# Extraction of the largest values in one block of eight units, with the ratios behind its first round and the clipping behind the block

## The chip, the cores and the metric

The kernel runs on one core of one Trainium2 chip. The metric is the device time of one execution in microseconds (us). PE is TensorE, DVE VectorE, ACT ScalarE, POOL GpSimd, SP SyncE. Each engine works through its own queue in order and waits at semaphores.

## The reference, cut to what matters

Four layers of a graph network run over 64 graphs of 256 nodes with 128 features, with one dense 256x256 adjacency for each graph; each layer adds to `x`:

```
h = relu(layernorm(x)); x = x + L0(h, adj)   # normalised adjacency, elu
h = relu(layernorm(x)); x = x + L1(h, adj)   # hyperbolic attention: logmap, expmap
h = relu(layernorm(x)); x = x + L2(h, adj)   # per edge: gelu(layernorm(m_j + m_i + b1)), summed with adj
h = relu(layernorm(x)); x = x + L3(h, adj)   # four stacked layers, row and column norms of adj
```

Two parts concern the change. L1 needs `_atanh(sn)` for every pair of nodes, with `sn` clipped below 1. The kernel takes it as a ratio by logarithms and exponentials: Ln of numerator and denominator, their difference, Exp of half of it, a clip, then Ln(1-u) and Ln(1+u). L2 sums over the edges of a node, and only about 3% of the entries of `adj` are not zero. So the kernel extracts for each node the list of its non-zero entries, eight at a time, and L2 runs over these slots and not over 256 neighbours.

## The kernel before, in words

Four graphs make a group, sixteen groups in all. A group has eight units: a unit is one half (128 rows) of one graph's adjacency. The main loop alternates two stages. `slots(g)` is the edge loop of L2 for group g, two slots in each turn. `mix(g)` does everything between two edge loops, each part for another group: the update after L2 of group g (flag `u`), L1 and the extraction for group g+1 (flag `l1`), L0 for group g+2 (`l0`), and L3 for group g-1 (`l3`). The order of the work on each engine is written out by hand in `mix`, once for each engine; nothing plans it.

The extraction is done sixteen times. This text calls these times block 0 to block 15. Blocks 0 and 1 stand in mixes without L3, block 15 in one without L0, the thirteen between in full mixes.

The extraction is `take_slots` (L1044) on DVE. One round, `eight` (L1054), takes the eight largest values of each unit (MAX8, L1056), finds their columns (L1059, a load of the values and FIND_INDEX8), copies the values away (L1060), overwrites them in `adj_x` (L1064, a load and MATCH_REPLACE8; not in the last round) and copies the columns away, cast to bf16 (L1065). A drain of DVE stands between these steps. The number of rounds is read from `n_slots`: three for fifteen blocks, four for block 3. It is the count of the first round, of a loop with a register bound, and of the last round.

Before, the extraction is made of two calls with four units each. In DVE's order (L1393 to L1402): the clamps of the last graph's pair terms (`clamp_pair`, `clamp_den`), then `take_slots(a, 0)` with all its rounds, then `ratios` (L1251), then `take_slots(a, 1, between=clip)`: its first round, `clip` (L1257), its further rounds. Then comes `index_ready`, then `layer0_z` (L997, from L1002 on), and `coefficients` (L1262).

- `ratios` is four subtractions 128x512 of two SBUF tiles (L1255), one for each graph. The one of graph b waits for ACT's Ln of that graph (L858) and for POOL's addition `total` (L584), which reads the same logarithms.
- ACT answers with Exp (L870, L871), and stands behind `keep_f` (L683) of L3 with it.
- `clip` is four operations 128x512 (L1260); each waits for one L870. After its own `keep_sd` copies (L679) ACT loads a table and waits for each `clip` before the Ln pair of that graph (L884, L885; "the artanh pair" below). Behind the four pairs ACT has a table load (L886), two `keep_f`, and `keep_index` (L699).
- PE's queue has at this place L3's products `l3_f(2, 0)` and `(2, 1)`, `turn_index` (L1702, matmuls L1710, waits for `index_ready`), `l3_f(2, 2)` (from L1612 on, waits for the first of those `keep_f`), `(2, 3)`, then `support` (L1692, waits for the result of `coefficients`, L1273).
- SP waits for `index_ready` to load `adj_x` for the next group.
- Later, `move` (L1310) on DVE waits for ACT's Tanh (L903), which stands in ACT's queue behind the last four `keep_sd`.

Of the kernel before, what the change touches and what calls it, by code (L numbers as in the profile page):

```python
# [32 lines left out]
GB = 4  # L33
# [177 lines left out]
UNITS = GB * NB  # L211
HALF = UNITS // 2
# [31 lines left out]
def network(nc, w, keep, out):  # L244
    with ExitStack() as stack:
# [11 lines left out]
        value = plan.sb("value", [P, UNITS, SLOTS])  # L257
# [3 lines left out]
        index = plan.view("index", [P, UNITS, CHUNKS * P], at, BF16)  # L261
# [66 lines left out]
        top = plan.sb("top", [P, UNITS, 8])  # L328
        top_at = plan.sb("top_at", [P, UNITS, 8], U32)
# [603 lines left out]
        def _(dve):  # L933
            v = nc.vector
# [62 lines left out]
            def layer0_z(z_):  # L997
                for b in range(GB):
                    dve.wait_ge(sem["out_made"], z_ * GB + (b // 2 * 2 + 2))
                    for k in range(NB):  # L1000
                        u = b * NB + k
                        v.scalar_tensor_tensor(z0[:, u], quarter(b)[:, k * P:(k + 1) * P],  # L1002
                                               norm[:, u:u + 1], bc["L0_gnn_b"][:], ALU.mult, ALU.add)
                dve.drain()
                for b in range(GB):
                    v.tensor_scalar(z0_low[:, of(b)], z0[:, of(b)], 0.0, None, ALU.min).then_inc(sem["z0_low_ready"], 1)
                v.scalar_tensor_tensor(normed[:], z0[:], 0.0, nodes(z_), ALU.max, ALU.add)
                dve.drain()
# [32 lines left out]
                v.tensor_scalar(n_slots[0:1, bass.ds(a, 1)], needed_g[:], 7.0, float(N), ALU.max, ALU.min)  # L1041
                dve.drain().then_inc(sem["slots_ready"], 1)

            def take_slots(a, part_, between=None):  # L1044
                units = range(part_ * HALF, (part_ + 1) * HALF)
                these = slice(part_ * HALF, (part_ + 1) * HALF)
                for b in range(part_ * 2, part_ * 2 + 2):
                    dve.wait_ge(adjx_in[b], a * 16 + 16)
                dve.wait_ge(sem["index_cleared"], a + 1)
                dve.sem_inc(keep["held"], 1)  # L1050
                n = dve.value_load(n_slots[0:1, bass.ds(a, 1)], min_val=7, max_val=N)
                full = dve.snap(((n + 1) // 2 * 2 + 10) // 8 - 1)

                def eight(r, more):  # L1054
                    for u in units:
                        v.max(top[:, u], adj_x[:, u])  # L1056
                    dve.drain()
                    for u in units:
                        v.max_index(top_at[:, u], top[:, u], adj_x[:, u])  # L1059
                    v.tensor_copy(value[:, these, bass.ds(r * 8, 8)], top[:, these])  # L1060
                    dve.drain()
                    if more:
                        for u in units:
                            v.match_replace(adj_x[:, u], top[:, u], adj_x[:, u], LOWEST)  # L1064
                    v.tensor_copy(index[:, these, bass.ds(r * 8, 8)], top_at[:, these])  # L1065
                    dve.drain()

                eight(0, True)
                if between:
                    between()  # L1070
                with dve.Fori(1, full) as r:
                    eight(r, True)
                eight(full, False)
# [68 lines left out]
            def mix(g, l1=True, l0=True, l3=True, u=True):  # L1142
                a, z_, t = g + 1, g + 2, g - 1
# [97 lines left out]
                def clamp_pair(b):  # L1241
                    dve.wait_ge(sem["pair_made"], a * GB + (b + 1))
                    v.tensor_scalar(pair[:, b, 0], bank_b[:, 0], -2.0, MIN_NORM, ALU.mult, ALU.max).then_inc(sem["square_ready"], 1)
                    dve.wait_ge(sem["square_ready"], a * GB + (b + 1))
                    v.tensor_tensor(pair[:, b, 1], pair[:, b, 0], bank_b[:, 1], ALU.add).then_inc(sem["pair_read"], 1)

                def clamp_den(b):
                    dve.wait_ge(sem["pair_read"], a * GB + (b + 1))
                    v.tensor_scalar(pair[:, b, 1], pair[:, b, 1], MIN_NORM, None, ALU.max).then_inc(sem["pair_clamped"], 1)

                def ratios():  # L1251
                    for b in range(GB):
                        dve.wait_ge(sem["ln_ready"], a * GB + (b + 1))
                        dve.wait_ge(sem["total_ready"], a * GB + (b + 1))
                        v.tensor_tensor(pair[:, b, 0], pair[:, b, 0], pair[:, b, 1], ALU.subtract).then_inc(sem["diff_ready"], 1)  # L1255

                def clip():  # L1257
                    for b in range(GB):
                        dve.wait_ge(sem["s_ready"], a * GB + (b + 1))
                        v.tensor_scalar(pair[:, b, 0], pair[:, b, 0], MAX_TANH, None, ALU.min).then_inc(sem["u_clipped"], 1)  # L1260
# [131 lines left out]
                if l1:  # L1392
                    clamp_pair(3)  # L1393
                    clamp_den(3)
                    take_slots(a, 0)
                    ratios()
                    take_slots(a, 1, between=clip)
                    dve.drain().then_inc(sem["index_ready"], 1)
                if l0:
                    layer0_z(z_)  # L1400
                if l1:
# [31 lines left out]
            for piece in (layer0_stats, layer0_eps, layer0_normed, layer0_scaled, layer0_z, layer0_moved, layer0_variance):  # L1433
                piece(0)
            mix(-1, l3=False, u=False)
            slots(0)
            mix(0, l3=False)
            with dve.Fori(1, GROUPS - 2) as g:
                slots(g)
                mix(g)  # L1440
# [493 lines left out]
```

## Time and profile before

| | |
|---|---|
| median of 3 runs | 4111.16 us (4110.72 to 4120.36) |
| the profiled execution's own time | 4122.07 us |
| its span, first to last instruction | 4120.2 us |
| busy PE / DVE / ACT / POOL | 87% / 83% / 68% / 52% |
| granted TensorE clock, mean | 0.923 |

The profiled execution lies 11 us above the median and 2 us above the highest of the three runs. A row of the time line gives the start in us from the span's start, the duration from the first start to the last end, engine, line, operation, output and inputs with their shapes, and the count; in brackets the idle time just before and what ended it.

### The profile page before, as it was taken

To read this page: it belongs to the slowest core of one execution; us is meant where nothing else is said; L and a number is where in the kernel's file an instruction comes from. 1 tells how busy PE (TensorE), PEld (TensorE's weight loads), DVE (VectorE), ACT (ScalarE), POOL (GpSimd) and SP (SyncE) were. 2 spreads that over 40 slices of the span, in tenths; PEclk is the share of its full clock that TensorE was granted. 3 is DMA by queue.
4 is the path that set the end of the run, shared out by engine and by line. 5 is a ranking of instruction groups with operands and counts; after the bars stand their busy time and mean duration, and the time that the engine had idled before them with its cause. 6 is when DMAs were issued, how large, how long until landed. Compare 5 with 4: busy or idle time off the path is not lost.

```text
span 4120.2 us, 103754 instructions
## 1 busy us (share of the span) xinstructions
PE 3577.9 (87%) x30351; PEld 3064.0 (74%) x30772; DVE 3411.6 (83%) x12271; ACT 2808.7 (68%) x6445; POOL 2154.7 (52%) x1987
## 2 busy tenths in 40 slices
PE   3494789889899999989899898998999898998998
PEld 2283778778787787868778786877878687786887
DVE  4788888898888888888888888888888888887840
ACT  2484776858667685866858686685858668595753
POOL 1182763719456382844728274572828447292730
PEclk7596889999998999989999898989989899999999
DMA  2000001000010100001010000101000010000000
GB/s 80 26 1 26 1 1 42 1 25 17 1 42 1 42 0 21 21 1 42 1 42 0 21 22 1 42 1 42 0 21 21 1 42 1 26 0 1 16 1 21
DMA packets 95517, 73.95 MB, mean 18 GB/s; under 512 B 7504, under 2 KB 95184, under 8 KB 95184
## 3 DMA queue, kind: packets, MB, share of 16 engines
q1 hardware_dynamic: 95184, 70.09, 5.6%
q8 instruction: 138, 2.26, 0.2%
q14 instruction: 195, 1.60, 0.1%
HBM read 61.68 MB, written 8.39 MB: 17 GB/s over the span
## 4 chain that ended last, share of the span: by engine, by line
PE 61%; DVE 16%; ACT 8%; issue 8%; POOL 3%; DVEq 2%; ACTq 0%; POOLq 0%; DMA 0%; SPq 0%
PE n_bank_d L1512 11%; PE n_bank_c L1501 9%; PE n_bank_b L1501 9%; PE n_bank_c L1598 9%; PE n_bank_d L1615 4%; PE n_bank_d L1616 4%; PE n_bank_d L1612 3%; PE n_bank_a L1484 3%; PE n_bank_b L1676 2%; DVE v_normed L987 1%; DVE v_normed L1149 1%; POOL v_z L517 1%; PE n_bank_a L1472 1%; DVE v_z L1109 1%; ACT v_pair L858 1%
## 5 line engine op out<-in xcount | busy, mean ns | idle before, releaser
L517 POOL TENSOR_TENSOR v_z<-v_z,all_bc_L_gnn_be 128x512 f32<-128x512 f32 x620 | 788.3, 1273 | 32.4 <-DVE v_z L1109 32.4
L1512 PE MATMUL n_bank_d<-v_diag,v_msg 128*128 128x128 f32 x4960 | 618.3, 278 | 25.1 <-ACT v_diag L756 25.1
L531 POOL TENSOR_TENSOR v_prstd<-v_pvar,all_neg_half 128x8 f32<-128x8 f32 x310 | 561.8, 1812 | 105.7 <-DVE v_pvar L1125 76.9
L1512 PEld LDWEIGHTS n_bank_d<-v_diag,v_msg 128*128 128x128 f32 x4960 | 577.0, 192 | 28.1 <-ACT v_diag L756 28.1
L756 ACT ACTIVATE v_diag<-all_ident,v_value 128x128 f32<-128x128 f32 x1860 | 573.6, 389 | 0.0
L1501 PEld LDWEIGHTS n_bank_b<-v_parts,v_onehot 128*128 128x128 bf16 x8208 | 473.4, 98 | 90.6 <-ACT n_bank_b L688 56.9
L1501 PE MATMUL n_bank_b<-v_parts,v_onehot 128*128 128x128 bf16 x8208 | 512.8, 219 | 26.2 <-ACT n_bank_b L688 26.1
L1501 PEld LDWEIGHTS n_bank_c<-v_parts,v_onehot 128*128 128x128 bf16 x7440 | 442.0, 100 | 108.9 <-ACT n_bank_c L688 64.6
L1501 PE MATMUL n_bank_c<-v_parts,v_onehot 128*128 128x128 bf16 x7440 | 479.8, 222 | 42.1 <-ACT n_bank_c L688 42.1
L1598 PE MATMUL n_bank_c<-all_l_wsd,v_fT 128*128 128x256 f32 x1792 | 457.8, 398 | 28.4 <-ACT v_adjT L673 25.9
L683 ACT ACTIVATE v_fT<-n_bank_d,all_l_c 128x256 f32<-128x256 f32 x256 | 120.0, 475 | 461.0 <-PE n_bank_d L1616 460.8
L1598 PEld LDWEIGHTS n_bank_c<-all_l_wsd,v_fT 128*128 128x128 f32 x1792 | 360.0, 201 | 69.9 <-issue 1.4
L751 ACT ACTIVATE v_msg<-v_z 128x512 f32<-128x512 f32 x620 | 384.0, 619 | 36.2 <-PE n_bank_d L1512 24.4
L1109 DVE SCALAR_TENSOR_TENSOR v_z<-n_bank_c,v_prstd,all_bc_L_gnn_g 128x128 f32<-128x128 f32 x1240 | 345.9, 345 | 66.5 <-PE n_bank_b L1501 36.1
L593 POOL TENSOR_TENSOR v_s_norm<-v_s_norm2c,v_half 128x8 f32<-128x8 f32 x16 | 28.1, 1758 | 710.7 <-DVE v_s_norm2c L1308 710.7
L692 ACT ACTIVATE v_spread<-n_bank_a 128x1024 bf16<-128x1024 f32 x342 | 345.0, 1009 | 60.0 <-PE n_bank_a L1484 42.9
L1109 DVE SCALAR_TENSOR_TENSOR v_z<-n_bank_b,v_prstd,all_bc_L_gnn_g 128x128 f32<-128x128 f32 x1240 | 346.9, 345 | 26.0 <-POOL v_prstd L531 25.8
L679 ACT ACTIVATE v_sd<-n_bank_c 128x512 f32<-128x512 f32 x256 | 151.0, 595 | 265.4 <-PE n_bank_c L1598 264.1
L1615 PE MATMUL n_bank_d<-v_adjT,v_sd 128*128 128x256 f32 x1024 | 327.9, 404 | 0.0
L1616 PE MATMUL n_bank_d<-v_adj_l,v_sd 128*128 128x256 f32 x1024 | 324.3, 400 | 0.0
L1099 DVE TENSOR_SCALAR v_onehot<-v_spread,v_node_of 128x1024 bf16<-128x1024 bf16 x684 | 307.8, 491 | 2.8 <-ACT v_spread L692 2.1
L1117 DVE BATCH_NORM_STATS2 v_pstats<-n_bank_b 128x6 f32<-128x256 f32 x620 | 234.2, 422 | 65.4 <-PE n_bank_b L1501 47.3
(283 smaller groups left out, 7435.5 us busy)
## 6 DMA issues: line engine op xcount, KB each, us to landing
v_adj_l<-in_adj SPq DMA_DIRECT2D x128, 256.0 KB, 3.6
v_adj_x<-in_adj SPq DMA_DIRECT2D x64, 256.0 KB, 3.5
v_ring<-in_x SPq DMA_DIRECT2D x16, 512.0 KB, 6.0
out_x<-v_xout SPq DMA_DIRECT2D x64, 128.0 KB, 1.9
w_wu<-in_L_gnn_wu SPq DMA_DIRECT2D x4, 192.0 KB, 2.5
all_W<-in_L_gnn_W SPq DMA_DIRECT2D x2, 128.0 KB, 4.0
w_raw<-in_L_gnn_ws SPq DMA_DIRECT2D x1, 192.0 KB, 3.0
w_raw<-in_L_gnn_wd SPq DMA_DIRECT2D x1, 192.0 KB, 3.2
```

The source lines that it names most:

```text
L517: nc.gpsimd.tensor_tensor(z[par][:, units], z[par][:, units], wide(bc["L2_gnn_be1"])[:, units], ALU.add).then_inc(sem["z_ready"], 1)
L531: nc.gpsimd.tensor_tensor(prstd[:], pvar[:], minus_half, ALU.pow).then_inc(sem["prstd_ready"], 1)
L692: nc.scalar.activation(spread[:], ps_spread, ACT.Copy).then_inc(sem["spread_kept"], 1)
L751: nc.scalar.activation(msg[par][:, units], z[par][:, units], ACT.Gelu).then_inc(sem["msg_ready"], 1)
L756: ins = nc.scalar.activation(diag[par][:, u], ident[:], ACT.Copy, scale=value[:, u, bass.ds(slot, 1)])
L1099: ins = v.tensor_scalar(onehot[:, par, k], spread[:], node_of[:, k:k + 1], None, ALU.is_equal)
L1109: ins = v.scalar_tensor_tensor(z[par][:, u], ps_m[par][:, u], prstd[:, u:u + 1], bc["L2_gnn_g1"][:], ALU.mult, ALU.mult)
L1501: ins = nc.tensor.matmul(ps_m[par][:, u], onehot[:, par, k, u * P:(u + 1) * P], parts[:, b * NB + k, t], start=False, stop=False, skip_gro ...
L1512: ins = nc.tensor.matmul(ps_agg[:, u // NB, (u % NB) * P:(u % NB + 1) * P], msg[par][:, u], diag[par][:, u], start=False, stop=False, skip ...
L1598: ins = nc.tensor.matmul(ps_l3[b % 2][:, k], fT[:, b, L3_SLOT[f], k * P:(k + 1) * P], keep["l3_wsd"][:, sum(L3_IN[:l]) + i, :], start=Fals ...
L1615: nc.tensor.matmul(acc, sd[:, b, k, 0:D], rowT[:, b, k], start=False, stop=False)
L1616: ins = nc.tensor.matmul(acc, sd[:, b, k, D:2 * D], colA[:, b, k], start=False, stop=k == NB - 1)
```

## The change

The two calls become one over all eight units. Each round now runs each of its steps over eight units, with the same number of MAX8, FIND_INDEX8 and MATCH_REPLACE8; its two copies move 64 elements a partition where they moved 32. There is one entry, one read of `n_slots` and one loop where there were two. `ratios` now runs behind the first round of the eight units, `clip` behind the whole block and behind `index_ready`. Nothing changes in the queues of ACT, PE, POOL and SP.

```diff
-            def take_slots(a, part_, between=None):
-                units = range(part_ * HALF, (part_ + 1) * HALF)
-                these = slice(part_ * HALF, (part_ + 1) * HALF)
-                for b in range(part_ * 2, part_ * 2 + 2):
+            def take_slots(a, between):
+                for b in range(GB):
                     dve.wait_ge(adjx_in[b], a * 16 + 16)
                 dve.wait_ge(sem["index_cleared"], a + 1)
                 dve.sem_inc(keep["held"], 1)
...
                 def eight(r, more):
-                    for u in units:
+                    for u in range(UNITS):
                         v.max(top[:, u], adj_x[:, u])
                     dve.drain()
-                    for u in units:
+                    for u in range(UNITS):
                         v.max_index(top_at[:, u], top[:, u], adj_x[:, u])
-                    v.tensor_copy(value[:, these, bass.ds(r * 8, 8)], top[:, these])
+                    v.tensor_copy(value[:, :, bass.ds(r * 8, 8)], top[:])
                     dve.drain()
                     if more:
-                        for u in units:
+                        for u in range(UNITS):
                             v.match_replace(adj_x[:, u], top[:, u], adj_x[:, u], LOWEST)
-                    v.tensor_copy(index[:, these, bass.ds(r * 8, 8)], top_at[:, these])
+                    v.tensor_copy(index[:, :, bass.ds(r * 8, 8)], top_at[:])
                     dve.drain()

                 eight(0, True)
-                if between:
-                    between()
+                between()
                 with dve.Fori(1, full) as r:
                     eight(r, True)
                 eight(full, False)
...
                     clamp_den(3)
-                    take_slots(a, 0)
-                    ratios()
-                    take_slots(a, 1, between=clip)
+                    take_slots(a, between=ratios)
                     dve.drain().then_inc(sem["index_ready"], 1)
+                    clip()
```

## Rows read from the trace of the kernel before

**Rows 1.** The page, part 4: the chain that ended last, by engine
```profile
PE 61%; DVE 16%; ACT 8%; issue 8%; POOL 3%; DVEq 2%; ACTq 0%; POOLq 0%; DMA 0%; SPq 0%
```
**Rows 2.** The waits, whole span: total us, times, longest
```profile
ACT v_s_th L903 <- DVE v_s_targ L1312: 34.7, 3, 17.3
```
**Rows 3.** Time line of DVE, block 2, first round of the first four units
```profile
599.50 1.41 DVE L1056 MAX8 v_top<-v_adj_x 128x8 f32<-128x256 f32 x4 [0.49 <-issue]
600.98 0.09 DVE L1059 MATCH_VALUE_LOAD v_top_at<-v_top,v_adj_x 128x8 f32 x1
...
602.81 0.09 DVE L1064 MATCH_VALUE_LOAD v_adj_x<-v_top,v_adj_x 128x8 f32 x1
...
604.39 0.18 DVE L1065 CAST v_index<-v_top_at 128x32 bf16<-128x32 uint32 x1
```
**Rows 4.** Time line of DVE, block 2, last round and what follows
```profile
633.12 1.41 DVE L1056 MAX8 v_top<-v_adj_x 128x8 f32<-128x256 f32 x4 [0.48 <-issue]
...
636.99 2.16 DVE L1002 SCALAR_TENSOR_TENSOR v_hn<-n_bank_a,v_norm,all_bc_L_gnn_b 128x128 f32<-128x128 f32 x8 [0.28 <-issue]
```
**Rows 5.** Time line of DVE, block 2, end of the first call, and ratios
```profile
613.76 1.19 DVE L1060 COPY v_value<-v_top 128x32 f32 x1
615.11 1.05 DVE L1065 CAST v_index<-v_top_at 128x32 uint32 x1 [0.17 <-issue]
616.31 2.50 DVE L1255 TENSOR_TENSOR v_pair<-v_pair 128x512 f32<-128x512 f32 x4
```
**Rows 6.** Time line of POOL, block 2
```profile
611.17 4.95 POOL L584 TENSOR_TENSOR v_total<-v_pair 128x512 f32<-128x512 f32 x4 [16.84 <-ACT v_pair L858]
```
**Rows 7.** Time line of ACT, block 2
```profile
636.23 0.63 ACT L884 ACTIVATE v_pair<-v_pair 128x512 f32<-128x512 f32 x1
...
641.82 0.84 ACT L683 ACTIVATE v_fT<-n_bank_d,all_l_c 128x256 f32<-128x256 f32 x2
```
**Rows 8.** Time line of PE, block 2
```profile
642.43 1.10 PE L1612 MATMUL n_bank_d<-v_fT,all_l_wn 128*128 128x256 f32 x4 [0.74 <-ACT v_fT L683]
...
647.69 1.95 PE L1692 MATMUL n_bank_b<-v_h,v_pair 128*128 128x129 f32 x16
```
**Rows 9.** Time line of DVE, block 2, the end of the coefficients
```profile
646.50 2.50 DVE L1273 TENSOR_TENSOR v_pair<-v_total,v_gate 128x512 f32<-128x512 f32 x4
```
**Rows 10.** Time line of DVE, block 0
```profile
130.65 1.41 DVE L1056 MAX8 v_top<-v_adj_x 128x8 f32<-128x256 f32 x4 [0.71 <-issue]
...
152.80 1.44 DVE L1260 TENSOR_SCALAR v_pair<-v_pair 128x512 f32<-128x512 f32 x4
...
163.82 2.16 DVE L1002 SCALAR_TENSOR_TENSOR v_hn<-n_bank_a,v_norm,all_bc_L_gnn_b 128x128 f32<-128x128 f32 x8 [0.19 <-issue]
```
**Rows 11.** Time lines of POOL, ACT, DVE and PE, block 3
```profile
844.73 4.97 POOL L584 TENSOR_TENSOR v_total<-v_pair 128x512 f32<-128x512 f32 x4 [15.46 <-ACT v_pair L858]
...
868.08 0.63 ACT L884 ACTIVATE v_pair<-v_pair 128x512 f32<-128x512 f32 x1
...
878.31 2.16 DVE L1002 SCALAR_TENSOR_TENSOR v_hn<-n_bank_a,v_norm,all_bc_L_gnn_b 128x128 f32<-128x128 f32 x8 [0.28 <-issue]
...
881.08 2.04 PE L1612 MATMUL n_bank_d<-v_fT,all_l_wn 128*128 128x256 f32 x4 [0.38 <-issue]
```
**Rows 12.** Time lines of POOL, ACT and DVE, block 4
```profile
1107.59 4.95 POOL L584 TENSOR_TENSOR v_total<-v_pair 128x512 f32<-128x512 f32 x4 [15.43 <-ACT v_pair L858]
...
1130.94 0.63 ACT L884 ACTIVATE v_pair<-v_pair 128x512 f32<-128x512 f32 x1
...
1131.72 2.16 DVE L1002 SCALAR_TENSOR_TENSOR v_hn<-n_bank_a,v_norm,all_bc_L_gnn_b 128x128 f32<-128x128 f32 x8 [0.27 <-issue]
```
**Rows 13.** Time lines of POOL, DVE and ACT, block 15
```profile
3761.88 4.95 POOL L584 TENSOR_TENSOR v_total<-v_pair 128x512 f32<-128x512 f32 x4 [19.11 <-ACT v_pair L858]
...
3765.79 3.40 DVE L1255 TENSOR_TENSOR v_pair<-v_pair 128x512 f32<-128x512 f32 x4
...
3784.10 0.63 ACT L884 ACTIVATE v_pair<-v_pair 128x512 f32<-128x512 f32 x1
```

## The prediction

> **What bounds the kernel now.** I read the page first, for the chain of work that ended last: PE carries 61% of it, DVE 16%, ACT 8% [rows 1]. No engine bounds the whole, so the change has to be read at its place. Second, the waits: of the sixteen Tanh that close a block's L1, only three waited for DVE, 34.7 us in all [rows 2]; in thirteen blocks DVE was ready when ACT had worked off its queue. The time lines say which three: blocks 0, 1 and 15. Third, the time lines of DVE, ACT, POOL and PE around one block, and the sixteen blocks laid side by side. Blocks 2 and 5 to 14 (eleven) repeat one pattern to about 0.1 us; block 2 stands for them. Blocks 0 and 1 are alike; 3, 4 and 15 are each their own.
>
> In block 2 the reader is to see a race between three queues. DVE ends the extraction at 636.71 (636.99 less the gap of 0.28) [rows 4]. ACT starts the artanh pairs at 636.23 and reaches the next `keep_f` at 641.82, 5.59 later [rows 7]. PE waits for it: it stood 0.74 until 642.43, and then ran through to `support` at 647.69 [rows 8]. DVE's first result for `support` was there at about 647.19 (646.50 plus 0.69, a quarter of the four in 2.50 with its tail) [rows 9], 0.5 ahead. So PE and ACT set the pace behind the block, and DVE keeps up with 0.5 to spare.
>
> **Part 1, the merged rounds.** A full round of four units takes 5.07: from 599.50 to the end of the cast at 604.57; MAX8 1.48, FIND_INDEX8 and the copy 1.83, MATCH_REPLACE8 1.58, cast 0.18 [rows 3]. One more unit costs 0.33 for MAX8 (four in 1.41, so 1.0 over three steps) and about 0.39 for each of the two pairs (1.58 over four). Eight units: 5.07 + 4 x 1.11 + 0.06 for the longer copies = 9.57, against 10.14 for two rounds of four. No row has a copy of 64 elements; it is bounded by 0.18, that of 32, and twice that, and I take the lower end and 0.03, as fixed cost rules rows this short; the upper end would add 1 us to a block. The last round takes 3.59 (633.12 to 636.71) [rows 4]: for eight units 3.59 + 4 x 0.72 + 0.05 = 6.52, against 7.18. The loop's exit costs 0.48 [rows 4]. What follows the ratios is then 9.57 + 0.48 + 6.52 = 16.57 with three rounds, 26.62 with four.
>
> Blocks 0 and 1 have no L3, the logarithms lie long ready, and DVE is what everyone waits for. From the first MAX8 to `layer0_z` is 33.17 now (130.65 to 163.82) [rows 10]. After: 9.57 + 2.40 (ratios, 0.60 each [rows 5]) + 16.57 + 1.44 (clips [rows 10]) + 0.19 = 30.17. That is 3.0 less in each. The clips come later there, but ACT's pairs (four in 4.2 by block 2's pace) are done before `coefficients` starts, 4.3 behind the last clip. Blocks 0 and 1: -6.0. If the drains and the loop's entry lay hidden already, it would be 0; that end goes into the range.
>
> **Part 2, the ratios move ahead of their inputs.** In block 2 the first round of eight ends at 599.50 + 9.57 = 609.07. POOL's additions, which the ratios wait for, start at 611.17 and run one after the other to 616.12, 1.24 apart [rows 6]; they hang on ACT's table load and Ln, which nothing here moves. So a stall of over 3 us opens on DVE where there was none, and then DVE is paced by POOL. Do the two engines run beside each other? In block 2 a copy and a cast beside the additions took 1.19 and 1.05 where the same forms take 0.17 and 0.18 [rows 3, 5], and in block 15 the four subtractions themselves, started 1.04 before the last addition ended (3766.83), took 3.40 where they take 2.50 [rows 5, 13]. DVE waited for the running addition to end. I take it so: the first subtraction waits until the second addition is done (2.48), runs 0.60, then they alternate: 2.48 + 0.60 + 1.24 + 0.60 + 1.24 + 0.60 + 0.60 = 7.36 from the first addition's start. Without such waits it would be 4.95 + 0.60 = 5.55.
>
> The Trainium skill says the same, in "SBUF — State Buffer", section "Who interferes with whom": a VectorE operation with two inputs in SBUF and a GpSimd operation that reads SBUF exclude each other for a whole instruction. By this rule the sum below holds; without it, it would be 5 us lower. The rows agree with it, for the cast and for the subtraction.
>
> Block 2: the ratios end at 611.17 + 7.36 = 618.53, now 618.81. What the stall costs, the merging and the absent clip waits give back. The extraction ends at 618.53 + 16.57 = 635.10, 1.6 earlier.
>
> **Part 3, the clip behind the block.** Its 1.44 come on top: `layer0_z` starts at 635.10 + 1.44 + 0.28 = 636.82, now 636.99: nothing won that counts. ACT's wait for the first clip takes the place of its wait for PE's copies: first clip done at 635.10 + 0.43 = 635.53, needed at 636.23 [rows 7], so 0.7 remains. That cover hides the move in these eleven blocks; if it is gone, each us costs one us of ACT, behind it of PE (`keep_f`, then `l3_f(2, 2)`, `support`, four `l3_sd`, the Tanh). `index_ready` comes 1.6 earlier, but `turn_index` stands behind L3 products in PE's queue, so no one is waiting; SP loads `adj_x` 1.6 earlier, needed a group later. Eleven blocks: 0 each.
>
> Where the cover is thinner:
> - Block 4. Ratios end 1107.59 + 7.36 = 1114.95, extraction 1131.52, first clip 1131.95; ACT would start at 1130.94 [rows 12]: 1.0 late. `layer0_z` at 1133.24, now 1131.72: 1.5 late, beyond DVE's 0.5. I take +1.5.
> - Block 15. Ratios end 3769.24, extraction 3785.81, first clip 3786.24, ACT now starts at 3784.10 [rows 13]: +2.1, for PE waits for `keep_f` there too.
> - Block 3, four rounds. Ratios end 852.09, extraction 878.71, first clip 879.14, where ACT starts at 868.08 now [rows 11], eleven us earlier. `keep_f` comes 5.59 after, ends at 885.15, and PE's product starts there and not at 881.08: +4.1. Part of it comes back, since these four matmuls took 2.04 after PE had stood still and 1.10 in block 2 [rows 8, 11]. DVE alone: `layer0_z` 880.43 for 878.31, +2.1. Between 2.1 and 4.1 I take +3.
>
> **Sum.** -6.0 + 0 + 1.5 + 2.1 + 3.0 = +0.6 us, on the profiled execution's 4122.07: 4122.7. That execution lies 10.9 over the median of the runs shown; carried over, 4111.16 + 0.6 = 4112. The edits cancel.
>
> **The rivals.**
> - No exclusion of the additions and subtractions. Ratios end 1.8 earlier. Blocks 4 and 15 then cost 0 and 0.3, block 3 1.3: sum -4.4, 4107. For it: only block 15 shows a late subtraction. Against it: 0.9 there is clear. Still "within".
> - DVE is the bound everywhere, and each block gives the 3.0 of block 0: -48, 4063. For it: DVE is 16% of the chain. Against it: rows 2 and 8, and the new stall of 3 us.
> - Slower: the clip comes late on ACT in all full blocks. Its place is the 0.7 before the first artanh pair. It decides as soon as the extraction ends over 0.7 later than worked out, through longer copies (the upper end, 1 us) and issue gaps of 0.5 at each of the steps as DVE shows them here and there. At 2 us later: 1.3 x 11 = 14, 2 x 3 = 6 in blocks 3, 4, 15, and 4 less won in blocks 0 and 1: +25, 4136. For it: the cover is thin, and thirteen blocks share it. Against it: each stage is scaled from its own row.
> - The change does not do what it says: drains and entries were hidden, blocks 0 and 1 give nothing: +6.6, 4118.
> - TensorE's granted clock falls at other places (2.04 against 1.10 for the same four matmuls is what it does): some 1 us a block, either sign.
>
> **How the numbers follow.** The forecast 0.60, with its own range 4105 to 4120; no exclusion 0.12; slower by a late clip 0.14; DVE the bound 0.05; nothing won 0.05; clock 0.04. About 0.3% (12 us) is what a measurement of this kernel can tell from no change. Slower by more: the 0.14 and 0.02 of clock and of the costs' upper ends, 0.16. Faster: 0.05 and 0.02, 0.07. Within: 0.77. The range reaches from the case without exclusion less the spread of the runs to the beginning of the late clip, 4102 to 4126.
>
> **What would show it.** DVE idle before L1255 of 3 us and more until POOL's L584 in the full blocks, and the four subtractions spread over some 6 us; none in blocks 0 and 1, which are 3 us shorter. MAX8 in rows of eight, 9.6 us a round. The first L884 unmoved against the `keep_sd` before it in block 2, late by 1 in block 4, by 2 in block 15, by 11 in block 3. Wrong would be: ACT idle before L884 in block 2 (then slower), the Tanh there earlier against the `keep_sd` (then faster), or subtractions of 0.69 each right behind their additions.

## The result, and the profile after

The changed kernel takes 4107.41 us (median of 12 executions, 4096.21 to 4114.05), the kernel before in the same rounds 4117.01. The ratio is 0.9974, its 95% interval 0.9966 to 0.9982: faster by 0.26%, some 10 us. I had forecast no change, 4112. The time lies in the range, and within the 0.3% that I called no change; but the interval of the ratio excludes 1, and where those 10 us come from is the question of what follows. That the number is only 5 off is in part luck: it rests on three runs with a median of 4111.16, and on the 4117.01 of the twelve my +0.6 would have given 4117.6. The profiled execution has a span of 4112.1 (before 4120.2), with the same mean clock of 0.923. Of all executions behind this text one, of the version with late ratios and 256 drains, was slow (4747.66 at a mean granted clock of 0.725), and no median or ratio below counts it.

The chain of the page, by engine, and the waits that answer to [rows 1, 2] (waited for: us in total, times, longest):

```profile
PE 58%; DVE 19%; ACT 7%; issue 7%; POOL 3%; DVEq 2%; POOLq 0%; ACTq 0%; DMA 0%; SPq 0%
```
```profile
DVE v_pair L1252 <- POOL v_total L584: 47.5, 14, 3.4
ACT v_pair L884 <- DVE v_pair L1257: 39.4, 6, 12.3
ACT v_s_th L903 <- DVE v_s_targ L1309: 30.6, 2, 15.4
...
PE n_bank_b L1706 <- DVEq L1393: 27.3, 3, 10.7
```

The first line is new: in each of fourteen blocks DVE stands 3.4 before the ratios until POOL's addition. The second was 1.5 in two waits; now ACT waits for the clip in six blocks. The lines of the changed kernel stand 2 to 5 lower in number than those of before, from the extraction on. Block 2 on DVE, against [rows 3 to 5]:

```profile
592.19 2.72 DVE L1054 MAX8 v_top<-v_adj_x 128x8 f32<-128x256 f32 x8 [0.58 <-issue]
...
598.15 0.18 DVE L1058 COPY v_value<-v_top 128x64 f32<-128x64 f32 x1
...
601.56 0.18 DVE L1063 CAST v_index<-v_top_at 128x64 bf16<-128x64 uint32 x1
605.15 5.63 DVE L1252 TENSOR_TENSOR v_pair<-v_pair 128x512 f32<-128x512 f32 x4 [3.40 <-POOL v_total L584]
610.70 2.70 DVE L1054 MAX8 v_top<-v_adj_x 128x8 f32<-128x256 f32 x8
...
627.04 0.20 DVE L1063 CAST v_index<-v_top_at 128x64 uint32 x1 [0.17 <-issue]
627.41 1.43 DVE L1257 TENSOR_SCALAR v_pair<-v_pair 128x512 f32<-128x512 f32 x4 [0.17 <-issue]
628.76 2.15 DVE L1002 SCALAR_TENSOR_TENSOR v_hn<-n_bank_a,v_norm,all_bc_L_gnn_b 128x128 f32<-128x128 f32 x8
```

One round of eight takes 9.55 (592.19 to 601.74; worked out as 9.57), and the copy of 64 elements costs what one of 32 did. POOL and ACT at the same place, ACT and PE in block 3, and ACT in block 5:

```profile
603.77 5.86 POOL L584 TENSOR_TENSOR v_total<-v_pair 128x512 f32<-128x512 f32 x4 [17.10 <-ACT v_pair L858]
```
```profile
627.88 0.63 ACT L884 ACTIVATE v_pair<-v_pair 128x512 f32<-128x512 f32 x1 [0.75 <-DVE v_pair L1257]
```
```profile
870.18 0.63 ACT L884 ACTIVATE v_pair<-v_pair 128x512 f32<-128x512 f32 x1 [11.00 <-DVE v_pair L1257]
```
```profile
870.38 1.84 PE L1706 MATMUL n_bank_b<-v_ident,v_index 128*128 128x128 bf16 x8 [6.16 <-DVEq L1393]
876.38 1.19 PE L1608 MATMUL n_bank_d<-v_fT,all_l_wn 128*128 128x256 f32 x2 [4.16 <-ACT v_fT L683]
```
```profile
1360.06 0.76 DVE L1257 TENSOR_SCALAR v_pair<-v_pair 128x512 f32<-128x512 f32 x2 [0.17 <-issue]
```
```profile
1361.46 0.63 ACT L884 ACTIVATE v_pair<-v_pair 128x512 f32<-128x512 f32 x1
```

The ratios end 7.01 after the first addition starts (610.78 less 603.77; worked out as 7.36), and the additions themselves are stretched from 4.95 [rows 6] to 5.86. In block 5 the first clip is done at about 1360.5, 0.95 ahead of ACT.

From the first MAX8 of a block to its Tanh, in the two profiled executions:

| block | before | after | measured | forecast |
|---|---|---|---|---|
| 0 | 59.59 | 57.07 | -2.5 | -3.0 |
| 1 | 59.40 | 56.42 | -3.0 | -3.0 |
| 3 | 71.52 | 75.04 | +3.5 | +3.0 |
| 4 | 62.08 | 63.40 | +1.3 | +1.5 |
| 15 | 62.55 | 65.92 | +3.4 | +2.1 |

These five sum to +2.7 where I had +0.6. In the steady blocks the time from the first addition to the Tanh is 51.98 for 52.09. So by its own edits the change gives nothing, as forecast, and the profiled execution is still 8 us shorter. Laid side by side over the sixteen blocks, these 8 are: -4.0 between Tanh and the transposes behind it (0.30 to 0.34 in each of the thirteen full blocks, 13.09 to 12.78), -7.2 between `first_features` and the first addition, +4.4 in the edge loops and ahead of block 0, +0.7 from the addition to the Tanh, -2.1 behind block 15. No instruction was changed in the first and the third of these places. The second holds the first round of eight, but the addition that ends it waits for ACT's Ln (L858) and not for that round.

What went there shows on DVE. Before, block 6, in `split` and in `move`:

```profile
1530.13 0.18 DVE L961 TENSOR_TENSOR v_whole<-v_whole,v_part 128x16 f32<-128x16 f32 x1
1530.74 0.17 DVE L958 CAST v_part<-v_whole 128x16 bf16<-128x16 f32 x1 [0.43 <-issue]
```
```profile
1641.79 0.17 DVE L1333 TENSOR_TENSOR v_s_ch<-v_s_num,v_s_rden 128x8 f32<-128x8 f32 x1
1642.18 0.17 DVE L1334 TENSOR_TENSOR v_s_cu<-v_s_cu,v_s_rden 128x8 f32<-128x8 f32 x1 [0.22 <-issue]
```

After, the same instructions:

```profile
1524.51 0.18 DVE L961 TENSOR_TENSOR v_whole<-v_whole,v_part 128x16 f32<-128x16 f32 x1
1524.76 0.18 DVE L958 CAST v_part<-v_whole 128x16 bf16<-128x16 f32 x1
```
```profile
1636.10 0.17 DVE L1330 TENSOR_TENSOR v_s_ch<-v_s_num,v_s_rden 128x8 f32<-128x8 f32 x1
1636.18 0.16 DVE L1331 TENSOR_TENSOR v_s_cu<-v_s_cu,v_s_rden 128x8 f32<-128x8 f32 x1
```

Two gaps in which DVE waited for nothing that the profile names are gone, in all thirteen passes of the loop. The merged calls have 30 instructions less a block, so the loop's body stands 60 instructions earlier in DVE's program, and what follows the extraction 90.

### The profile page after: what moved, and what is told of

Same layout as the page of the kernel before. It is cut to its first block, busy times and chain, and to the rows that moved or that the text cites. A ratio compares the mean times of both kernels' runs of the same rounds, so it can differ in the third digit from the quotient of the medians.

```text
span 4112.1 us, 103279 instructions
## 1 busy us (share of the span) xinstructions
PE 3576.3 (87%) x30351; PEld 3063.1 (74%) x30772; DVE 3400.8 (83%) x12173; ACT 2804.6 (68%) x6445; POOL 2169.4 (53%) x1987
## 3 DMA queue, kind: packets, MB, share of 16 engines
q14 instruction: 182, 1.49, 0.1%
## 4 chain that ended last, share of the span: by engine, by line
PE 58%; DVE 19%; ACT 7%; issue 7%; POOL 3%; DVEq 2%; POOLq 0%; ACTq 0%; DMA 0%; SPq 0%
PE n_bank_d L1508 11%; PE n_bank_c L1497 9%; PE n_bank_b L1497 9%; PE n_bank_c L1594 8%; PE n_bank_d L1611 4%; PE n_bank_d L1612 4%; PE n_bank_d L1608 3%; PE n_bank_a L1480 3%; DVE v_normed L987 2%; PE n_bank_b L1672 2%; DVE v_normed L1146 1%; POOL v_z L517 1%; DVE v_top_at L1057 1%; PE n_bank_a L1468 1%; DVE v_z L1106 1%
```

## The experiments

All times are medians, each with the recorded ratio to the kernel before run beside it (it can lie 0.001 from the quotient of the two medians) and the 95% interval of that ratio. "Steady" are the full blocks without 3 and 4.

**Undo the merging alone.** Each round in two groups of four:

```diff
-                    for u in range(UNITS):
-                        v.max(top[:, u], adj_x[:, u])
+                    for part_ in range(2):
+                        these = slice(part_ * HALF, (part_ + 1) * HALF)
+                        units = range(part_ * HALF, (part_ + 1) * HALF)
+                        for u in units:
+                            v.max(top[:, u], adj_x[:, u])
...
+                        v.tensor_copy(value[:, these, bass.ds(r * 8, 8)], top[:, these])
```

> The changed kernel with every round run as two groups of four units (MAX8, drain, FIND_INDEX8, copy, drain, MATCH_REPLACE8, cast, drain, and the same again); the place of ratios and clip stays. Theory (merging saves 0.57 us a full round and 0.66 in the last, and the clip has 0.9 us of cover on ACT in the steady blocks): blocks 0 and 1 longer by 1.8 each; what follows the ratios 1.2 longer, so the first L884 waits for the clip and comes 0.3 late in nine steady blocks and 1.2 late in blocks 2 and 8; blocks 3, 4, 15 by 1.8, 0.4, 1.2; sum +12, 4119. Rival (fixed costs were hidden): 0, 4107. Second rival (DVE bounds every block): 1.8 x 16 = +29, 4136.

4134.38 us, 1.004 (1.0027 to 1.0053), 27 above the changed kernel. In block 9:

```profile
2349.58 0.63 ACT L884 ACTIVATE v_pair<-v_pair 128x512 f32<-128x512 f32 x1 [0.51 <-DVE v_pair L1260]
```

The theory's mechanism holds, its size was too small. From the ratios to the clip it is 18.03 for 16.64 (+1.39 against 1.2), and the first L884 comes 0.5 late in the steady blocks (0.3 forecast). The Tanh comes another 0.5 late, through DVE itself, which I had left out: in block 9 it waits 0.36 for DVE's `v_s_targ` (L1312). Block 4 is 3.8 longer for 0.4 forecast: behind its late clip PE stood 2.89 for `v_fT`, and the 5.49 us from there ran at a granted clock of 0.50, where the same stretch of block 9, after 1.24 of standing, had 1.00. And from Tanh to the transposes it is 13.14 again, as in the kernel before: 0.36 x 13 = 4.7 of the 27 are no cost of the rounds.

**The clip ahead of the last round.**

```diff
                 with dve.Fori(1, full) as r:
                     eight(r, True)
+                last()
                 eight(full, False)
...
-                    take_slots(a, between=ratios)
+                    take_slots(a, between=ratios, last=clip)
                     dve.drain().then_inc(sem["index_ready"], 1)
-                    clip()
```

> The changed kernel with the clip ahead of the last round and not behind the block. Theory (in blocks 3, 4 and 15 the clip behind the block holds up ACT's artanh pairs by 11, 1.5 and 2.2 us): the first L884 comes back to its place of before in blocks 4 and 15 and to within 4.5 us in block 3; the segments to Tanh are shorter by about 1.3 (block 4), 2 to 3 (block 15), 2 (block 3), nothing in the others; sum -5, 4102. Rival (DVE itself, layer0_z, holds up these three blocks, the clip only follows): 0, 4107.

4101.73 us, 0.9962 (0.9949 to 0.9975): the 4102 forecast. From the first MAX8 to the Tanh, against the changed kernel: block 3 73.18 (75.04 with the clip behind; -1.9 for -2), block 15 62.44 (65.92; -3.5 for -2 to -3), block 4 63.00 (63.40; -0.4 for -1.3), -5.8 in all. In block 3 ACT waits 2.67 and not 11:

```profile
866.62 0.64 ACT L884 ACTIVATE v_pair<-v_pair 128x512 f32<-128x512 f32 x1 [2.67 <-DVE v_pair L1258]
```

**The ratios behind the loop.**

```diff
                 eight(0, True)
-                between()
                 with dve.Fori(1, full) as r:
                     eight(r, True)
+                between()
                 eight(full, False)
```

> The changed kernel with the ratios behind the loop of the rounds, ahead of the last round, and the clip behind the block. The ratios then run long after POOL's additions: no wait (3.4 us now) and no alternation (5.6 us now, 2.5 then), so in blocks of three rounds the extraction ends 6.5 earlier. Theory (PE and ACT set the pace in the full blocks): these 6.5 give nothing in the ten steady ones; blocks 4 and 15 lose their late clip (-1.3, -3); block 3 with four rounds gets its Exp 7 us late and its clip 7 us earlier, -2.5; sum -7, 4100. Rival (DVE sets the pace): 6.5 x 13 = -85. Second rival (the port: the wait and alternation are no loss of DVE's but of POOL's additions, which stay slowed): additions still 5.9 and not 4.95.

4096.21 us, 0.9952 (0.9937 to 0.9966). Block 2, DVE and POOL:

```profile
613.14 2.50 DVE L1252 TENSOR_TENSOR v_pair<-v_pair 128x512 f32<-128x512 f32 x4 [0.57 <-issue]
```
```profile
604.14 4.96 POOL L584 TENSOR_TENSOR v_total<-v_pair 128x512 f32<-128x512 f32 x4 [17.03 <-ACT v_pair L858]
```

Apart from each other the two take 2.50 and 4.96, beside each other 5.63 and 5.86. So the stretching is of these two against each other, and that rival of mine (additions slow anyway) is out. DVE's first clip lies 4.8 to 6.5 ahead of ACT in the steady blocks, and the Tanh does not follow by that: from the first addition it comes after 51.98 in blocks 5 and 11, as in the changed kernel, and after 50.3 in the other nine, where the quickest of the changed kernel take 51.3. PE and ACT set the pace for most of it, and -85 is out too. From the first MAX8 to the Tanh block 3 gives 4.4 (2.5 forecast), block 15 3.5 (3), and block 4 nothing (63.50 for 63.40, 1.3 forecast).

**DVE's later code moved by padding.** 60 drains at the very start of DVE's program, where it waits for the weights from 3.8 to 26.2; a drain takes 0.04 there. (The line numbers of kernels with drains are 2 higher.)

```diff
         @block.vector
         def _(dve):
+            for _ in range(60):
+                dve.drain()
             dve.wait_ge(stored, 1)
```

> The changed kernel with 60 drains more at the very start of DVE's program, where it waits some 22 us for the weights: they cost nothing there, but every later instruction stands 60 places further on, as it stands in the kernel before at the top of the loop body (two blocks of 30 instructions ahead of it). Theory (DVE's issue gaps hang on the place in the instruction stream): the gap of 0.43 ahead of the casts L958 is back in the thirteen blocks of the loop; the one ahead of the product behind L1330 isn't (it needs 90); the time between the changed kernel's and 4 us more. Rival (the gaps went because of DVE's timing against other engines): no gap comes back, the time stays 4107.

4119.61 us, 1.0004 (0.9995 to 1.0012). Sixty instructions that cost nothing where they stand take the whole gain away. Block 6:

```profile
1529.44 0.17 DVE L960 CAST v_part<-v_whole 128x16 bf16<-128x16 f32 x1
1530.05 0.17 DVE L963 TENSOR_TENSOR v_whole<-v_whole,v_part 128x16 f32<-128x16 f32 x1 [0.43 <-issue]
```

The gap is back with the same 0.43, one step ahead of where the kernel before has it. The other is not back: 12.78 from Tanh to the transposes. The forecast was right on both gaps, and too low on the time (up to 4 us more; it is 12).

**Thirty more** (`range(90)`).

> The changed kernel with 90 drains more at the start of DVE's program, 30 more than the run with 60. Theory (place in the instruction stream): the gap of 0.22 (0.30 between the starts) ahead of the product behind L1330 in move is back in the thirteen blocks of the loop, so from Tanh to the transposes 13.09 and not 12.78; the gap in the split of the first features, which the run with 60 had one instruction ahead of where the kernel before has it, moves 30 instructions forward, out of the first split. Rival (gaps hang on DVE's timing): 12.78 stays, the gap stays in the split.

4116.62 us, 1.0003 (0.9994 to 1.0012). 13.13 from Tanh to the transposes, and block 6 in `move`:

```profile
1640.03 0.17 DVE L1328 TENSOR_SCALAR v_s_denc<-v_s_den 128x8 f32<-128x8 f32 x1
1640.62 0.20 DVE L1330 RECIPROCAL v_s_rden<-v_s_denc 128x8 f32<-128x8 f32 x1 [0.42 <-issue]
```

The other gap has left `split`; it stands ahead of L1151 (0.51). Between there and the place of the run with 60 lie 30 instructions, the reads of the accumulator counted. The gap keeps its place in the stream, and the code is pushed past it.

**Do 256 instructions more bring the picture back?** The changed kernel with 256 drains, and the kernel before with 196, which puts its loop where the changed kernel has it.

> The changed kernel with 256 drains more at the start of DVE's program (10 us, hidden in the 22 us of its wait for the weights). Theory (the gaps come at every 256th instruction: those of the kernel before at L958 and behind L1330 lie 462 written instructions apart, with some 50 hidden loads between about 512; an instruction packet on the page has 2.26 MB / 138 = 16.4 KB): the gaps are where the changed kernel has them, none at L958, 12.78 from Tanh to the transposes, and the time is the changed kernel's, 4107. Rival (no such period, each shift is its own): other gaps, a time of its own up to 4120.

> The kernel before with 196 drains more at the start of DVE's program: with a period of 256 its loop body then stands as the changed kernel's does at the top of its loop (60 places earlier). Theory (4 to 5 of the changed kernel's gain of 10 are the gaps, another 4 the granted clock that went with them): the gap at L958 is gone, the time falls from 4117 by 4 to 10, 4107 to 4113, with no round merged and nothing moved. Rival (the gain is the merging's): 4117.

With 256: 4108.56 us, 0.9985 (0.9976 to 0.9995), and in block 6 the same gaps at the same instructions as in the changed kernel. The kernel before with 196: 4109.55 us, 0.9988 (0.9979 to 0.9997); neither gap, 12.78 from Tanh to the transposes. Its block 6 in `split`:

```profile
1524.45 0.18 DVE L963 TENSOR_TENSOR v_whole<-v_whole,v_part 128x16 f32<-128x16 f32 x1
1524.70 0.17 DVE L960 CAST v_part<-v_whole 128x16 bf16<-128x16 f32 x1
```

Both come out as the theory says, but they cannot tell a period of 256 from a shorter one of which 256 is a multiple. An edit that moves and merges nothing gives half of the gain or more: 0.9988, where the changed kernel has 0.9974, and with 256 drains, in the same rounds, 0.9985.

**How thin is the clip's cover?** The changed kernel with 2 us more of DVE ahead of the clip:

```diff
                 eight(full, False)
+                for u in range(6):
+                    v.max(top[:, u], adj_x[:, u])
```

> The changed kernel with six MAX8 more behind the last round, ahead of index_ready and clip: 6 x 0.33 = 2.0 us of DVE. Theory (ACT's artanh pairs have 0.9 of cover in the steady blocks, DVE's coefficients some 1.2 ahead of support): the first L884 waits for the clip in all blocks, 1.1 late in nine, 2.0 in blocks 2, 8, 3, 15, 0 and 1; the Tanh 1.1 to 1.6 late; sum 9 x 1.4 + 6 x 2.0 + 1.2 (block 4) = +26, 4133. Rival (PE's pace hides it): 5 at most. Second rival (DVE bounds all): 2.0 x 16 = +32.

4143.15 us, 1.0058 (1.0044 to 1.0073): 36 more for 2 us of DVE. The first L884 waits in every block, in block 9 by 1.24:

```profile
2360.61 0.63 ACT L884 ACTIVATE v_pair<-v_pair 128x512 f32<-128x512 f32 x1 [1.24 <-DVE v_pair L1259]
```

It comes 1.15 to 1.20 later than the 25.0 behind the first addition that it has in most steady blocks of the changed kernel (1.1 forecast). The excess over the forecast lies behind it: in blocks 4 to 7 the Tanh comes another 1.7 to 2.7 late. TensorE's granted clock goes with it. Block 5, then block 9, from PE's product for `l3_f(2, 2)` on, ahead of which it had stood 1.90 and 1.96 (stretch, its length, PE busy, granted clock, DMA):

```profile
1386.46:1391.01 4.55, 4.55 (x13) 0.62 0.00 0
2366.81:2371.36 4.55, 4.55 (x21) 1.00 0.00 0
```

The rival with 5 is out. The total lies nearest to the second rival's 32, but its place is wrong: at L884 a steady block is not 2.0 late.

**The kernel before at the changed kernel's place behind the extraction** (196 replaced by 166), the changed kernel once more, and the version with late ratios at 256.

> The kernel before with 166 drains more at the start of DVE's program: behind the extraction its loop body then stands as the changed kernel's does (90 places earlier in a period of 256). Theory (gaps at every 256th instruction; the changed kernel's gain is their place): no gap at L958 and none ahead of L1334, 12.78 from Tanh to the transposes, the one that was there comes in node_stats with 0.15; median within 4 us of the changed kernel run beside it. Rival (the merged rounds themselves gain): 4 to 10 above it.

> The changed kernel once more, to stand beside the other two in the same rounds. All theories: 4107, 0.997 of before.

> The version with the ratios behind the loop, with 256 drains more at the start of DVE's program. Theory (period 256): the same gaps and the same time as without them, 4096 (one run of 6 executions stands behind that), 0.995 of before. Rival (4096 was the granted clock's doing): up to 4107.

The kernel before: 4100.77 us, 0.9948 (0.9934 to 0.9961). The changed kernel: 4108.41, 0.9973 (0.9962 to 0.9985), as the first time. The late ratios: 4088.82, 0.9918 (0.9903 to 0.9933). So the kernel before, with nothing but drains in front, is 8 us faster than the changed one in the same rounds. My theory said within 4, its rival 4 to 10 slower: both missed, the rival with the wrong sign. The gaps at L958 in `first_features` and ahead of L1334 are gone, as forecast, but it has others, which the theory had not named: in the second call of `split`, and between two rounds of the extraction, where the kernel before with 196 drains stands 0.23:

```profile
1537.84 0.17 DVE L960 CAST v_part<-v_whole 128x16 bf16<-128x16 f32 x1 [0.41 <-issue]
```
```profile
1575.25 1.41 DVE L1058 MAX8 v_top<-v_adj_x 128x8 f32<-128x256 f32 x4 [0.58 <-issue]
```

Between these two places lie 128 records of DVE's trace, drains and register operations counted.

What goes with its lower time is TensorE's granted clock. The stretches from 30 to 50 and from 66 to 76 us behind `first_features`, block 7, of the changed kernel, then of the kernel before with 166 (stretch, its length, PE busy, granted clock, DMA):

```profile
1793.11:1813.11 20.00, 17.45 (x56) 0.66 0.00 0
1829.11:1839.11 10.00, 7.39 (x31) 0.83 0.00 0
```
```profile
1790.53:1810.53 20.00, 16.77 (x59) 0.76 0.00 0
1826.53:1836.53 10.00, 8.16 (x42) 1.00 0.00 0
```

A full block comes in two lengths. From `first_features` to the first addition it takes 64.3 to 65.2 or 63.1 to 63.6 in these two and the kernel before, and from there to ACT's first L884 25.0 or, where the clip is ready, 23.35, as more or less of it runs at 1.2 GHz and not 2.4. The profiled executions have this many short first halves (under 64) among thirteen full blocks:

```
before 2        changed 4, again 2        late ratios 10, at 256: 6
before+196: 5   before+166: 7             changed+60: 2, +90: 1, +256: 7
```

Over the twelve executions of the changed kernel, time and mean granted clock go together (4114.05 at 0.923, 4096.21 at 0.931; correlation -0.95, 2.3 us for each 0.001).

## Why the prediction was right in its steps and wrong in its sum

- **What bounds the kernel.** Right in the long blocks: the late ratios give DVE 6.5 there, and the Tanh does not move. In a short block it comes 1.0 earlier by them (50.29 for 51.27 from the first addition), so in the changed kernel DVE bounds the short ones.
- **Merged rounds.** Right: 9.55 for 9.57; from the ratios' end to the end of the extraction 16.46 for 16.57 (610.78 to 627.24). Blocks 0 and 1 gave 2.5 and 3.0 for 3.0.
- **Ratios ahead of their inputs.** Right: the stall of 3.4, the alternation of 7.01 for 7.36. By the page "SBUF — State Buffer" of the Trainium skill (section "Who interferes with whom") the two exclude each other for a whole instruction; the rows agree, for both sides are stretched beside each other, and neither is when they are apart.
- **Clip behind the block.** Right in the long blocks: the cover is 0.95 for 0.7, and 2 us more of DVE come through as 1.15. Right in 3, 4 and 15, where 15 was mis-sized (+3.4 for +2.1). But "block 4" was no case of its own. It is the short kind of block, and in the changed kernel's trace blocks 2 and 8 are short too; ACT waits 0.75 for the clip there (its row above). From the first addition to the Tanh a short block takes 51.3 where the kernel before with 166 has 50.4. The late clip alone does not account for these 0.9. With the clip ahead of the last round the first L884 of a short block waits for nothing, and the Tanh comes at 51.4 all the same: `support` waits for DVE's coefficients, and the Tanh for `v_s_targ` (block 5 of that version):

```profile
1370.47 2.03 PE L1688 MATMUL n_bank_b<-v_h,v_pair 128*128 128x129 f32 x16 [0.50 <-DVE v_pair L1271]
```
```profile
1386.41 0.21 ACT L903 ACTIVATE v_s_th<-v_s_targ 128x8 f32<-128x8 f32 x1 [0.27 <-DVE v_s_targ L1310]
```

So DVE as a whole is late there, by the stall and the alternation behind the early ratios; without them the 0.9 are gone (50.3). The more blocks the clock makes short, the more the change costs: an estimate of 7 x 0.9 = 6 for the seven short ones of that run. The 8 that divide the two kernels hold more than this, for their shares of short blocks differ too (seven, and two in the changed kernel beside it).

- **`index_ready`: "no one is waiting".** Said of the eleven blocks. Block 3, where it does not hold, had no such term: `turn_index` waited 5.77 for it before and 6.16 after. It stands where it stood (34.4 behind the first addition for 34.1), and what costs is the 4.16 behind it, for which PE stands for `keep_f`, late by the clip.
- **The sum.** This step failed (+0.6 forecast, -10 measured): it took every instruction not named in the diff as unmoved. "Part 1" counts the drains and entries removed by their own time only. That 30 instructions less a block shift all of DVE's later code had no term; "issue gaps ... as DVE shows them here and there" stood only in the slower rival, as if they were scattered and could only grow. Measured: 0.30 to 0.34 a block behind the Tanh, 4.0 in the thirteen; 0.36 between the starts in `split`; and with them another share of short and long blocks.
- **The rival of the clock** ("some 1 us a block, either sign", 0.04) came nearest to what shows beside it, and was underrated. Its step is 1.5 + 1.65 = 3.1 us for a block that turns from long to short in the kernel before, and 1.5 + 0.7 = 2.2 in the changed one, which gains less in the second half.

At equal places the change as a whole shows no gain: what the merged rounds give, the new places of the ratios and the clip take back. With the loop at the same place the changed kernel is even with the kernel before (4108.56 and 4109.55), and with the same place behind the extraction it is 8 us slower (4108.41 and 4100.77). What stays open: why a place of the code brings more short blocks, and how much of each time is the clock's doing. The two gaps themselves account for 4.0 behind the Tanh and at most 0.36 x 13 = 4.7 in `split` (part of which a wait behind it takes back); the rest goes with the clock, and no run set the clock. Nor do the intervals cover all that varies: the late ratios gave 0.9952, and 0.9918 with 256 drains.

The version with late ratios beats both kernels, in both of its runs. It keeps the merged rounds, and takes away the stall, the alternation and, in all blocks but 0 and 1, the late clip.

## What to carry to other kernels

An edit that changes the number of instructions on an engine moves everything behind it; before a gain of a few tenths of a percent is put down to the edit, run a version with harmless padding ahead of the loop, and compare at equal places. A cover is to be read from the block in which the waiting engine is earliest, not from the typical one. DVE's four subtractions beside POOL's four additions cost both (5.63 for 2.50, and 5.86 for 4.96); behind the loop, where POOL was idle, the same subtractions took 2.50.

## What the runs showed of the hardware that was not expected

- DVE has gaps of 0.2 to 0.5 us at fixed places of its instruction stream (0.43 in `split`), and 256 instructions more bring back the same picture. The places lie closer than 256, though: the two rows of the kernel before with 166 drains are 128 records apart. The pages of the profile agree with 128. With 256 drains more, queue q14 has 184 instruction packets for 182, of 8.2 KB each (1.49 MB / 182), while q8 keeps its 138: two packets for 256 instructions, 64 bytes for each. In the trace a packet of q14 starts behind each of the three gaps in `first_features`: at 1531.21 in the kernel before, 1530.53 with 60 drains, 1526.64 with 90, 0.5 to 0.9 after the instruction behind the gap. That the gap is a wait for instructions is the reading that fits all of this; no row names it.
- The Trainium skill describes such a fetch in "Runtime: NRT & Kernel Launch", section "Instruction fetch mechanics": blocks of 16 KiB, 256 instructions, the crossing "mostly hidden". The 64 bytes agree; in DVE's rows the step is half of such a block. Hidden it is not where DVE sets the pace with short operations: 0.30 to 0.36 each time.
- Twelve us, 0.3% of the kernel, hang on where 60 drains stand, and eighteen in the kernel before on 166 (4118.89 to 4100.77 in the same rounds).
- The copy of 64 elements a partition takes 0.18, as the one of 32.
